# AdaLN transformer block with sparse attention on one core: a new begin, the input prepared one slot ahead, and new orders on all engines

## What is computed

```python
h = _layernorm(x) * (1 + ca) + sa
x = x + ga * attention(h)          # 16 heads of 32; three branches, mixed by a softmax gate
h = _layernorm(x) * (1 + cb) + sb
x = x + gb * ffn(h)
# attention: q, k = rope(h @ Wq), rope(h @ Wk); v = h @ Wv; then the sum over branches of gate * softmax @ values
#   comp: 64 compressed blocks of 16 keys (causal);  sel: 2 blocks of 8 keys chosen by the mean score
#   win:  the last 128 keys (causal);  out @ Wo + bo
# ffn: h @ base_W.T + base_b + shared low-rank part + six routed low-rank parts, top 2 of 6 by a router
```

## Time and profile before

| | us |
|---|---|
| median of three runs | 2371.56 |
| the profiled execution | 2375.0 |
| its span | 2373.1 |
| TensorE busy | 2145.7 (90%) |
| VectorE busy | 1749.7 (74%) |
| ScalarE busy | 1340.7 (56%) |
| GpSimd busy | 788.2 (33%) |
| begin, head, end | 59.8, 92.2, 223.9 |
| one loop batch | 280.0 |
| clock of TensorE, mean | 0.96 of 2.4 GHz |

### The profile page before, as it was taken

How to read it: one execution, slowest core, us unless ns; L and a number is a source line. 1 busy time by engine, 2 the same in 40 slices (tenths; PEclk the granted TensorE clock), 3 DMA queues, 4 the chain that set the end, 5 groups by cost and what they waited for, 6 DMA issues and landing times.

```text
span 2373.1 us, 48974 instructions
## 1 busy us (share of the span) xinstructions
PE 2145.7 (90%) x17944; PEld 1427.3 (60%) x17944; DVE 1749.7 (74%) x4740; ACT 1340.7 (56%) x4701; POOL 788.2 (33%) x780
## 2 busy tenths in 40 slices
PE   4888999899998999989999899989999899997887
PEld 0665666566665666656665566656666566664454
DVE  3456888768886788768887688866887678875776
ACT  1244666556665566646656566655666556663664
POOL 0333333343333233333332433324333423333221
PEclk9998999999999999989999899999999999997989
DMA  6010000200011000110001100020001100011000
GB/s 233 19 40 15 23 28 24 68 22 28 28 32 63 28 24 28 46 49 19 28 28 41 54 28 24 23 76 24 22 25 45 50 28 28 24 46 45 19 19 19
DMA packets 48892, 89.64 MB, mean 38 GB/s; under 512 B 6760, under 2 KB 6760, under 8 KB 48656
## 3 DMA queue, kind: packets, MB, share of 16 engines
q1 hardware_dynamic: 39440, 69.74, 9.6%
q10 hardware_dynamic: 9216, 16.78, 1.9%
HBM read 69.68 MB, written 16.83 MB: 36 GB/s over the span
## 4 chain that ended last, share of the span: by engine, by line
PE 63%; DVE 22%; ACT 6%; issue 5%; POOL 2%; DMA 1%; SPq 0%; DVEq 0%; ACTq 0%; POOLq 0%
PE ps_m L702 9%; PE ps_o L634 7%; PE ps_m L506 6%; PE ps_m L667 5%; PE ps_m L507 5%; PE ps_m L508 5%; PE ps_s L628 4%; PE ps_t L610 4%; DVE ps_s L1548 4%; ACT pw L1033 3%; PE ps_m L684 3%; DVE wmax L1553 3%; PE ps_s L597 3%; PE ps_s L586 3%; PE ps_m L705 2%
## 5 line engine op out<-in xcount | busy, mean ns | idle before, releaser
L1033 ACT ACTIVATE pw<-ps_s,wmax 128x128 f32<-128x128 f32 x1024 | 360.3, 382 | 168.5 <-DVE wmax L1553 168.4
L506 PE MATMUL ps_m<-w_hi,h_hi 128*128 128x512 f32 x768 | 374.0, 487 | 35.1 <-DVE rbf L1520 18.9
L1043 ACT ACTIVATE pw<-pw,wden 128x128 f32<-128x128 f32 x1024 | 313.2, 401 | 5.0 <-DVE wden L1563 4.8
L507 PE MATMUL ps_m<-w_lo,h_hi 128*128 128x512 f32 x768 | 309.7, 403 | 0.0
L508 PE MATMUL ps_m<-w_hi,h_lo 128*128 128x512 f32 x768 | 308.5, 402 | 0.0
L1067 ACT ACTIVATE pT<-ps_s 80x512 f32<-80x512 f32 (+7 forms) x240 | 141.9, 591 | 255.6 <-PE ps_o L634 155.7
L1311 POOL TENSOR_TENSOR h_lo<-hT,h_hi 128x512 fp32r<-128x512 f32 x57 | 72.3, 1268 | 540.4 <-ACT h_hi L993 540.4
L702 PE MATMUL ps_m<-wbt_s,h2T 128*128 128x512 f32 x512 | 249.0, 604 | 0.0
L667 PE MATMUL ps_m<-wo_s,aT 128*128 128x512 f32 x512 | 247.8, 609 | 0.0
L1574 DVE COPY_PREDICATED pT<-keep_prev,ps_t 128x512 f32<-128x512 uint32 x224 | 164.3, 733 | 94.2 <-PE ps_t L610 90.2
L1033 ACT ACTIVATION_READ_ACCUMULATOR pw<-ps_s,wmax 128x1 f32 x1024 | 226.6, 221 | 0.0
(11 more groups left out here) (187 smaller groups left out, 4341.9 us busy)
## 6 DMA issues: line engine op xcount, KB each, us to landing
xa<-x_in SPq DMA_DIRECT2D x65, 256.0 KB, 3.0
xc<-x_in SPq DMA_DIRECT2D x64, 256.0 KB, 2.8
out<-t ACTq DMA_DIRECT2D x64, 256.0 KB, 2.0
wo_s<-wo_in SPq DMA_DIRECT2D x8, 1024.0 KB, 6.3
wbt_s<-wbt_in SPq DMA_DIRECT2D x8, 1024.0 KB
gbc<-gate_rows SPq DMA_DIRECT2D x24, 256.0 KB, 5.4
pw<-wmod_in SPq DMA_DIRECT2D x3, 1024.0 KB, 5.5
pT<-wmod_in SPq DMA_DIRECT2D x3, 1024.0 KB, 5.3
```

Of the source, the lines that this page charges most:

```text
L506: pe_.matmul(ps[:], h_hi[:, c, :], w_hi[:, col, c, :], start=(c == 0), stop=False)
L507: pe_.matmul(ps[:], h_hi[:, c, :], w_lo[:, col, c, :], start=False, stop=False)
L1033: ins = act.activation(pw[:, hw, :], ps_w[:, j, i, 1, :], ACT.Exp, bias=wmax[:, hw:hw + 1], accum_out=wden[:, 0, hw:hw + 1])
L1043: act.activation(pw[:, hw, :], pw[:, hw, :], ACT.Copy, scale=wden[:, 2, hw:hw + 1]).then_inc(wn_ok, 1)
```

## The change

It does five things.

1. Begin. `d_first` counts two loads (cT and the first constants). The other 16 small loads are issued by ScalarE and counted by a semaphore of their own, d_rest, which is waited for ahead of the first gate logits and by the other engines ahead of the head. Only MOD0 and MOD1 stand ahead of the head; MOD2, MOD5, MOD3, MOD4 and the second transpose are parts of head tiles 0 to 6 in a bank of their own, and so are VectorE's tables and gate rows. Each of the three projection weights has its own semaphore and is split as it lands. wa_s is waited for at the first turn.
2. HT, `h_scaled` and `split_h` of tile t+1 stand at the end of the slot of tile t, not at the beginning of their own.
3. Rows of x for stage C are loaded ahead of the weights (`load_xc` ahead of `load_gates` and of `load_feed`).
4. `t_spare(t, g)` is false for all of tile 0.
5. New orders and banks on all engines. In GpSimd's first slot, scale_feed and residual_in now stand ahead of the rotation of Q; in its turn, scale_out stands ahead of cs_subtract; deviation_a stands behind weigh_keys in slots. No operation of the loop is added or taken away.

The core of the diff (PE, ACT, POOL and VectorE parts of the slot and the first slot; the turn, the end and the head change likewise):

```diff
@@ orders of the banks
-SLOT_ORDER = [("HT", 1), ("Y", 0), ("Q", 1), ("K", 1), ("QT", 0), ("G", 0),
-              ("H2T", 0), ("Z", 0), ("KT", 1), ("F", 0), ("ZT", 1), ("V", 1)]
+SLOT_ORDER = [("Y", 1), ("Q", 0), ("K", 1), ("QT", 0), ("G", 0), ("H2T", 0),
+              ("Z", 1), ("F", 0), ("KT", 1), ("ZT", 1), ("V", 1), ("HT", 0)]
...
 def t_spare(t, g):
-    return t > 0 or g % 2 == 0
+    return t > 0
@@ SP
-                if t > 1:
+                if T > 1:
                     sp.wait_ge(r_ok, R_STEPS * (T - 2) + 2)
...
                     load_xa(NT * (b + 1) + NT - 2, (b + 2) % B, 0)
+                    load_xc(NT * (b + 1), b + 1, 0)
                     load_gates(b + 1)
                     sp.wait_ge(*m_full_at("loop", b, "Y", NT - 1))
                     load_out()
+                    load_xc(NT * (b + 1) + 1, b + 1, 1)
                     sp.wait_ge(*m_full_at("loop", b, "F", NT - 1))
                     load_feed()
@@ PE, slot
                 cs_scores(b, s)
-                transpose_h(seg, b, t, Ta)
                 output(seg, b, t, [0])
                 window_scores(b, s, 0)
                 output(seg, b, t, [1, 2, 3])
                 project(seg, b, t, "Q", 0, [0, 1, 2, 3])
                 window_scores(b, s, 1)
-                project(seg, b, t, "K", 1, [0])
                 transpose_window(b, s, 0)
+                project(seg, b, t, "K", 1, [0, 1])
                 transpose_rot(seg, b, t, Ta, "QT", ra, 1)
-                project(seg, b, t, "K", 1, [1, 2])
                 gate_logits(seg, b, t, [0, 1, 2, 3])
-                project(seg, b, t, "K", 1, [3])
+                project(seg, b, t, "K", 1, [2, 3])
                 transpose_h2(seg, b, t)
...
+                project(seg, b, t, "V", 2, [0, 1, 2])
+                transpose_h(seg, b, t + 1, Ta + 1)
                 transpose_window(b, s, 3)
-                feed(seg, b, t, [NC])
-                cs_values(b, s, 1)
+                project(seg, b, t, "V", 2, [3])
@@ PE, first_slot
                 window_scores(b, 1, 0)
-                transpose_h(seg, b, t, Ta)
-                window_scores(b, 1, 1)
                 project(seg, b, t, "Q", 0, [0])
...
                 cs_values(b, 0, 0)
+                window_scores(b, 1, 1)
                 transpose_cs(b, 0, 2)
+                cs_values(b, 0, 1)
                 transpose_cs(b, 0, 3)
-                cs_values(b, 0, 1)
                 cs_values(b, 0, 2)
+                project(seg, b, t, "K", 1, [2, 3])
+                cs_values(b, 0, 3)
                 transpose_rot(seg, b, t, Ta, "QT", ra, 1)
...
                 cs_scores(b, 1)
@@ PE, head
+                mod_part(t)
+                project(seg, b, t, "Q", 0, [0, 1, 2])
@@ ACT, slot
-                h_scaled(seg, b, t, "HT", hT, mod_a, moda_ok, ba + 1)
-                split_h(seg, b, t, Ta)
                 window_exp(b, s, 0)
+                window_norm(b, s, 0)
                 cs_exps(b, s)
-                window_norm(b, s, 0)
                 copy_qT(seg, b, t)
...
+                h_scaled(seg, b, t + 1, "HT", hT, mod_a, moda_ok, ba + 1)
+                split_h(seg, b, t + 1, Ta + 1, t)
                 copy_out(b, s)
+                copy_v(seg, b, t)
                 store(seg, b, t)
-                copy_v(seg, b, t)
@@ ACT, end of the setup's part in a head tile
                 h_scaled(seg, b, t + 1, "HT", hT, mod_a, moda_ok, 1)
+                mod_part(t)
+                split_h(seg, b, t + 1, t + 1, t)
                 copy_v(seg, b, t)
-                split_h(seg, b, t + 1, t + 1, t)
@@ POOL, first_slot
                 cs_normalise(b, 0)
+                scale_feed(b)
+                residual_in(b, t)
                 rotate(seg, b, t, Ta, "Q", ra)
-                residual_in(b, t)
-                scale_feed(b)
+                cs_subtract(b, 1)
                 rotate(seg, b, t, Ta, "K", kr)
-                cs_subtract(b, 1)
@@ POOL, slot
                 rotate(seg, b, t, Ta, "K", kr)
-                deviation_a(Ta + 1)
                 weigh_keys(seg, b, t, Ta)
+                deviation_a(Ta + 1)
+                split_h(Ta + 1)
@@ VectorE, slot
                 residual(seg, b, t)
                 window_weights(b, s, 0)
+                ln_scale(x1[:], mvc, vec, xc[:, t % 2, :], lnc, lncp, NT * b + t)
                 rope(seg, b, t, "Q")
                 window_max(b, s, 1)
                 cs_factor(b, s)
-                ln_scale(x1[:], mvc, vec, xc[:, t % 2, :], lnc, lncp, NT * b + t)
                 gates_soft(seg, b, t, Ta, 0)
@@ VectorE, first_slot
+                cs_factor(b, 0)
                 window_max(b, 1, 0)
+                rope(seg, b, t, "Q")
+                window_max(b, 1, 1)
+                rope(seg, b, t, "K")
                 window_weights(b, 1, 0)
...
@@ VectorE, end_slot
                 residual(seg, b, t)
+                window_weights(b, s, 0)
                 ln_scale(x1[:], mvc, vec, xc[:, t % 2, :], lnc, lncp, NT * b + t)
-                window_weights(b, s, 0)
```

613 lines of the change are left out of this document (336 added, 277 removed).

## The result

The changed kernel takes 2366.94 us (median of 12 runs, 2364.24 to 2368.88), the kernel before 2372.78 (12 runs, 2370.47 to 2377.58): a ratio of 0.9975, 95% interval 0.9966 to 0.9984, so 5.8 us less. The forecast was 17 less. The profiled execution has a span of 2362.4 against 2373.1.

What follows compares the result with a forecast made beforehand. It took TensorE to bound the loop, with only its gaps and the clock lost in them to win. Terms -29 + 21 + 2 - 7.5 + 0 - 5 + 1.5 = -17 from 2371.6 gave 2355 us, range 2303 to 2393.

Steps and rivals of the forecast that it cites:

- Begin -32, head +3: Begin and head: first projection 32 us earlier, at 32 to 33; head tiles 3 longer; together -29.
- Middle slots +21: 42 middle slots: each 0.5 us longer, +21 in all, bounds -8 to +42.
- HT at the end: Middle slots: the next tile's input transposes, moved to the slot's end, cost their own 0.5 us a slot.
- the ln_scale term: Middle slots: ln_scale placed ahead of the rope delays Q's transposes by 0.5 us.
- the gap at the gate product: Middle slots: TensorE stands about 0.9 us for ScalarE's copy of Q's transposes in the same bank.
- First slots: First slots: six get 0.3 us longer each (+2), with an 8 to 9 gap before Q's transposes; batch 0's gains 7.5.
- rival D: First slots: GpSimd's wait behind wb_s isn't absorbed, six slots cost 6 us each, +34, 2389; chance 0.22.
- Turns 0: Eight turns: no change in all, bounds -8 and +8 us.
- End -3.5: End: -5 us from its first slot and a denser rest, +1.5 from six later slots.
- B: Rival on the slots: their orders fit better, -0.7 us a slot instead of +0.5, 2305; chance 0.20.
- C: Rival on the slots: VectorE's time counts, 0.95 us out of each of 42, -40, 2315; chance 0.05.
- E: Rival on the begin: it starts no earlier than 45, -17 instead of -29, 2367 us; chance 0.06.

Runs made afterwards that it cites:

- select_beside: Changed kernel with compress chunk 3 directly ahead of select_values in the turns and the window's third values behind both: 2365.01 us, ratio 0.9958.
- select_router: select_beside plus, on ScalarE in the turns, the router's exponential ahead of the copy of the compressed values: 2361.89 us, ratio 0.9951 to the kernel before.

## Why the prediction was right and wrong

1. **Begin -32, head +3.** The first projection came at 32.07, where 32 to 33 stood. The head was mis-sized: it grew by 6.3 (89.58 to 95.85), not by 3. The six tile distances are 14.67, 13.64, 13.45, 14.37, 14.38 and 12.29 against 12.57: half a product costs 0.9 to 1.1, not nothing, and a whole one 1.8. (The first tile can't be read so: its 14.37 before had a mean clock of 0.86, its 14.67 after had 1.00.) So 2.7 of the 29 were missing. VectorE's share of a head tile, put at about 8, is 5.8 by the row quoted for it, which changes nothing.
2. **Middle slots +21.** The term that was furthest off: +2. Of its parts, HT at the end was right for slots 2 to 5 (+0.3 to +0.7), the ln_scale term was nil, and the gap at the gate product is 0.69, but covering it gave back 0.0 to 0.2. The step that failed here is the use of one slot, that of 578.88, for all six: the last two got 0.8 and 0.3 shorter. The bounds held (-8 to +42); the length of "32.5 to 33" holds for three of the six places.
3. **First slots.** Batch 0's -7.5 was exact. For the others, wb_s landing after 15.07, the queue behind it, the gap and the fallen clock came as written, with a gap of 6.4 to 7.4 for 8 to 9. Measured +1.15 a slot, forecast +0.3: within the bounds, and far from rival D's 6. The prediction had seen that the 8 gained ahead of the gap go in it, and took that as given; 8.6 a slot, the whole gain of the new order, hung on the place of one operation in GpSimd's queue.
4. **Turns 0.** This is the step that failed: +18, beyond its own bound of 8, and by its own last sentence a sign of being wrong (turns that differ by over 1; they differ by 1.9 and 4.8). "Scale_out now runs beside small VectorE operations" was set at nothing by a sentence, without asking which operations; they are on the chain to the choice. Nor did the prediction count the products that ran at the same time before, or ScalarE's order around the router. The experiments put 1.15 of the 1.90 of the seven turns on the selection's place and ScalarE's order and 0.2 on scale_out. The rest is the size of the 0.55 for which TensorE waits at a turn's output product for V's copy, in whose bank it now stands (argued, not tried; in the turn from 685.65):

```profile
686.93 1.98 PE L683 MATMUL ps_m<-wo_s,aT 128*128 128x512 f32 x4 [0.55 <-ACT v_s L1059]
```

   In the first turn the clock has 2.0 of the 4.8: one order takes 34.20 with 6.8 us at 1.2 GHz, as the kernel before had (the run select_beside), and 36.33 with 13.7 (the run select_router). Of the other 2.8, 0.6 is scale_out (selection 5.76 behind the importances instead of 6.35), about 1.1 the importances' later place in TensorE's order, and the rest stays open.
5. **End -3.5.** The profile has -3.8, but that is luck: most executions don't have it. Its first slot got 3.0 shorter (47.6 to 44.6), where 5 stood. What follows took 180.3 before, 179.5 in this profile, and 182.4 to 183.9 in ten of the twelve experiments on the changed kernel (+2 to +3.6), where +1.5 stood.

So two errors of 18 and 19 us with opposite signs met in the sum, and the -17 was nearer to the truth than its parts, by luck. What is left of the miss in the two profiles is the head (2.7) and the first slots (4.9), 7.6 in all, from -17 to about -10 (-10.8 in the table); the medians, with -5.8, add the 5 by which the two profiled executions lie off them, of which the end is a part. The chances that it gives to "faster" (0.20, 0.05 and 0.40) add up to 0.65, not to 0.63. Of the rivals, B (the slots are the same on the mean, and only one place in six got more than 0.7 shorter), C and E (first projection at 32) are wrong, and D's mechanism is there at a fifth of its price.
